# Last stage of a two-layer graph network kernel: operands turned and copied two groups ahead of their products instead of one

## The chip, the cores and the metric

The kernel runs on one core of one Trainium2 chip. The metric is the device time of one launch in microseconds (us). A core has five engines that run their own queues in order: TensorE (PE in the profile, with its weight loads as PEld), VectorE (DVE), ScalarE (ACT), GpSimd (POOL) and SyncE (SP). They meet through semaphores. In this kernel SP and POOL mostly issue DMA transfers: SP the plain ones, POOL the indirect ones, which gather or scatter 128 rows of 96 floats by a list of row numbers.

## The reference

A graph has 50000 nodes with 96 features each and 25000 edges, sorted by their target node `dst`. Two layers follow each other; each adds to its input and normalises.

```python
# layer 0: gated messages, summed per target, then a node update
edge_input = concat([x[src], edge_attr_32])
messages = gelu(edge_input @ mW1 + mb1) @ mW2 + mb2
gates = sigmoid(gelu(edge_input @ gW1 + gb1) @ gW2 + gb2)
aggregated = segment_sum(messages * gates, dst, N)
h = x + gelu(concat([x, aggregated]) @ uW1 + ub1) @ uW2 + ub2
x1 = layernorm(x + layernorm(h) * ln_g + ln_b)

# layer 1: attention over edges, 8 heads of 12 features
K, Q, V = x1 @ Wk + bk, x1 @ Wq + bq, x1 @ Wv + bv
E = edge_attr_96 @ We + be
score = K[src] * Q[dst] / sqrt(12) * E
score = exp(clip(sum over each head of score, -5, 5))
wV = segment_sum(V[src] * score, dst, N)
Z = segment_sum(score, dst, N)
out = layernorm(x1 + wV / (Z + 1e-6))
```

All is float32.

## The kernel before

The kernel has three stages. The edge stage gathers `x[src]` and makes the gated messages; the update stage makes `x1` for all nodes and stores it, with `layernorm(x1)` as the output of nodes that no edge reaches; the last stage, the one that changes, does layer 1 for the edges. It takes 49 groups of 512 edges (`EGROUPS`, four tiles of 128 each, `EJ`). Since edges are sorted by target, a running sum that a mask resets at each new target gives the segment sums, and the row of a target's last edge is scattered to `out`.

POOL's queue is one long list of indirect transfers, 196 of each of five kinds: gathers of `x` (L355), scatters to `agg_d` (L364), gathers of `x1` by target (L380), and, in the last stage, gathers of `x1` by source into a ring of `AHEAD` = 24 groups in the tile `node_work` (L392, `gather_src`) and scatters to `out` (L399, `scatter_out`). In the last stage POOL first issues the gathers of groups 0 to 7, then the scatter of group 0, and from there one gather group and one scatter group in turn: the scatter of group g-7 stands behind the gather of group g (`BEHIND` = 7). After the gather of group 48 the scatters of groups 42 to 48 are left. A gather of group g waits until PE has turned group g-4 (`LEAD`); a scatter of group g waits for `fin_made`, the end of ACT's four operations L667 on that group.

One step of the last stage is called here by its number i, the group whose products it makes. All engines have a function `attend_step(i)` for it.

- PE: wait until ACT has copied all three operands of group i; products K (L545), Q (L546), E (L549) and V (L552), where V waits until the scan of group i-1 is done (`cscanned`); turning the scan of group i-1 back (L556); turning the source rows of group i+1 (L418 with `node_work`) once their gather has landed; the head sums of group i (L538); turning the target rows (L418 with `wide`) and the edge attributes (L418 with `ea`) of group i+1.
- ACT: K with its bias (L663); the four final operations of group i-3 (L667); the three copies of the turned operands of group i+1 out of PSUM (L673, into `nT` or `einT`, the two sets of `opT`); the exponential of the scores of group i (L676), which so stands behind the copies.
- DVE: products with Q (L934) and E (L946), the clip (L969), the score times V (L986), the scan (L992), and between them the division by Z (L952 to L961), the statistics (L980) and the root of groups i-1 and i-2; last `cshift` (L999), which releases L667.
- SP: for each group g the load of its edge attributes `ea` (L327) and then of its mask (L330). The load of `ea` for group g waits until PE has turned group g-2 (there are two buffers), the mask of group g waits for the scan of group g-2. SP's queue is in order, so the load of `ea` for group g+1 stands behind the mask of group g.

PSUM banks 0, 1 and 2 hold the turned source rows, target rows and edge attributes of one group only.

Of the kernel before, what the change touches and what calls it, by code (L numbers as in the profile page):

```python
# [32 lines left out]
EGROUPS = -(-E // EROWS)  # L33
# [11 lines left out]
XSLOTS = 4  # L45
AHEAD = 24
EDGE_LEAD, LEAD, BEHIND = 8, 4, 7
# [27 lines left out]
def build(nc, x, src, dst, ea32, ea96, mW1, mb1, mW2, mb2, gW1, gb1, gW2, gb2, uW1, ub1, uW2, ub2,  # L75
          ln_g, ln_b, Wq, bq, Wk, bk, We, be, Wv, bv, ident_c, heads_c, spare_c, bounds_c, out):
    with ExitStack() as ctx:
# [84 lines left out]
        def two_banks(b):  # L162
            return ps[:, b:b + 2, 0:EJ * D]


        nTf = nT[0:D, :, :].rearrange("p s c -> p (s c)")
        opT = [[nTf[:, 0:512], nTf[:, 512:1024], nTf[:, 1024:1536]],
               [nTf[:, 1536:2048], einT[0:D, 0, :], einT[0:D, 1, :]]]

# [58 lines left out]
        def slot_total(slot):  # L228

            return 16 * len(range(slot, NGROUPS, 2))  # L230
# [185 lines left out]
        def _(pe):  # L416
# [123 lines left out]
            def attend_step(i):  # L540
                s = i % 2
                if 0 <= i < EGROUPS:
                    pe.wait_ge(opsT_copied, i * 3 + 3)
                    xsT, xdT, eaT = opT[s]
                    pe.matmul(ps[0:D, 3, :], Wks[:, :], xsT, start=True, stop=True).then_inc(k_summed, 1)  # L545
                    pe.matmul(ps[0:D, 4, :], Wqs[:, :], xdT, start=True, stop=True).then_inc(q_summed, 1)  # L546
                    if i >= 1:
                        pe.wait_ge(clipped, i)
                    pe.matmul(ps[0:D, 5, :], Wes[:, :], eaT, start=True, stop=True).then_inc(e_summed, 1)  # L549
                    if i >= 1:  # L550
                        pe.wait_ge(cscanned, i)
                    pe.matmul(ps[0:DH, 6, :], Wvs[:, :], xsT, start=True, stop=True).then_inc(v_summed, 1)  # L552
                if i >= 1:
# [3 lines left out]
                    m.then_inc(seg_turned, 1)  # L557
                if i + 1 < EGROUPS:
                    n = i + 1
                    pe.wait_ge(x1s_gathered[n % 2], of_group(n))  # L560
# [11 lines left out]

            for i in range(-1, EGROUPS + 1):
                attend_step(i)
# [3 lines left out]
        def _(act):  # L578
# [80 lines left out]
            def attend_step(i):  # L659
# [4 lines left out]
                if i >= 3:  # L664
# [4 lines left out]
                    o.then_inc(fin_made, 1)  # L669
                if i + 1 < EGROUPS:  # L670
                    for b in range(3):
                        act.wait_ge(ops_turned, i * 3 + 4 + b)
                        act.activation(opT[1 - s][b], ps[0:D, b, :], ACT.Copy).then_inc(opsT_copied, 1)  # L673
                if 0 <= i < EGROUPS:
# [3 lines left out]
            for t in range(2):  # L678
                act.wait_ge(x1_stored[t], slot_total(t))
            for i in range(-1, EGROUPS + 3):  # L680
                attend_step(i)
# [353 lines left out]
```

## Time and profile before

| | |
|---|---|
| median of 3 runs | 1260.01 us (1258.67 to 1260.13) |
| the profiled execution | 1260.09 us, span of the core 1258.3 us |
| PE busy | 959.2 us, 76% |
| DVE busy | 935.4 us, 74% |
| ACT busy | 690.8 us, 55% |
| POOL busy | 945.6 us, 75%, 984 instructions |
| first gather of the last stage (POOL, L392) | 756.52 us |
| first turning in the last stage (PE) | 762.92 us |
| first scatter to `out` (POOL, L399) | 796.49 us |

The times of rows are microseconds from the span's start. Busy shares are averages over three stages; the last stage fills the last 500 us. Idle time of an engine is listed with what ended it; "issue" as what ended it means that the engine waited for nothing that the profile shows. A row that is marked x4 stands for four instructions of one kind in direct succession.

### The profile page before, as it was taken

The numbers are of one execution on the slowest core, as the hardware profiler recorded it, in microseconds if no ns is written. First come the engines' busy times: TensorE is split into PE (matmuls) and PEld (weight loads), VectorE is DVE, ScalarE is ACT, GpSimd is POOL, SyncE is SP. The second block draws the span as 40 slices with busy tenths as digits, with TensorE's granted clock in tenths as the row PEclk, the third lists the DMA queues.
The fourth block names the chain that finished last, engine by engine and source line by source line (L and its number), as shares of the span: only waits on it lengthen the run. The fifth ranks groups of instructions, "written<-read, shape, count | busy, mean of one in ns | idle before, by whom it ended". The sixth has DMA issues, their size and how long they took to land. (4 is left out here: it accounts for less than half of the span.)

```text
span 1258.3 us, 18104 instructions
## 1 busy us (share of the span) xinstructions
PE 959.2 (76%) x4628; PEld 580.5 (46%) x4628; DVE 935.4 (74%) x4244; ACT 690.8 (55%) x1522; POOL 945.6 (75%) x984
## 2 busy tenths in 40 slices
PE   5789999989988898888887006887777786787780
PEld 2334444448777677777675003443333333333330
DVE  3435454547999999999999604999777877787873
ACT  2445555533788888888888703555444443444441
POOL 6677777777777777777777777777777777777777
PEclk9889999999999999999998558999888888788875
DMA  5975555444677777777775432333222322222320
GB/s 126 198 194 182 178 183 182 104 140 128 201 219 226 234 224 222 229 235 220 224 230 175 153 78 65 96 88 86 74 74 74 74 74 74 74 75 73 82 59 29
DMA packets 131946, 178.07 MB, mean 142 GB/s; under 512 B 75125, under 2 KB 76852, under 8 KB 131841
## 3 DMA queue, kind: packets, MB, share of 16 engines
q1 hardware_dynamic: 97741, 130.13, 35.5%
q0 software_dynamic: 31360, 46.18, 14.9%
q10 hardware_dynamic: 2740, 0.60, 0.3%
q8 instruction: 36, 0.59, 0.2%
q14 instruction: 69, 0.57, 0.1%
HBM read 101.31 MB, written 77.56 MB: 142 GB/s over the span
## 5 line engine op out<-in xcount | busy, mean ns | idle before, releaser
L399 POOL DMA_INDIRECT out<-wide,put_at x196 | 192.9, 984 | 59.7 <-issue 57.6
L364 POOL DMA_INDIRECT agg_d<-wide,put_at x196 | 191.2, 976 | 61.9 <-issue 55.5
L355 POOL DMA_INDIRECT wide<-in_x,src_i x196 | 185.5, 946 | 69.5 <-issue 58.1
L392 POOL DMA_INDIRECT node_work<-agg_d,src_i x196 | 188.1, 960 | 59.7 <-issue 57.0
L380 POOL DMA_INDIRECT wide<-agg_d,dst_at x196 | 187.7, 957 | 60.1 <-issue 49.7
L635 ACT ACTIVATE node_work<-node_work,nshift,nscale 128x96 f32<-128x96 f32 x392 | 145.7, 454 | 75.7 <-DVE nshift L885 75.6
L673 ACT ACTIVATE nT<-ps 96x512 f32<-96x512 f32 x99 | 57.0, 592 | 169.5 <-PE ps L418 169.4
L418 PE MATMUL ps<-ident,node_work 128*96 128x128 f32 x196 | 32.9, 293 | 133.7 <-DMA node_work<-agg_d,src_i 133.7
L508 PE MATMUL ps<-uW2s,nT 97*128 97x96 f32 x784 | 98.8, 279 | 45.1 <-ACT nT L653 45.1
L767 DVE SCALAR_TENSOR_TENSOR ps<-hidden,ps 96x512 f32<-96x512 f32 x49 | 33.9, 692 | 128.4 <-ACT hidden L616 128.4
L508 PEld LDWEIGHTS ps<-uW2s,nT 97*128 97x128 f32 x784 | 91.6, 192 | 55.1 <-ACT nT L653 55.1
L641 ACT ACTIVATE node_work<-node_work,nscale 128x96 f32<-128x96 f32 x392 | 112.7, 361 | 0.0
L667 ACT ACTIVATE wide<-yc,cshift,cscale 128x96 f32<-128x96 f32 x196 | 75.5, 456 | 62.7 <-DVE cshift L999 62.2
L850 DVE BATCH_NORM_STATS2 bn<-ps 128x6 f32<-128x96 f32 x392 | 99.3, 258 | 11.3 <-PE ps L508 11.2
L523 PEld LDWEIGHTS ps<-centre,einT 96*128 96x128 f32 x784 | 95.2, 192 | 25.0 <-issue 25.0
L864 DVE SCALAR_TENSOR_TENSOR node_work<-node_work,nscale 128x96 f32<-128x96 f32 x392 | 101.9, 305 | 4.3 <-ACT node_work L635 4.3
L518 PE MATMUL ps<-einT,uW1x 96*96 96x512 f32 x196 | 97.2, 619 | 0.0
L523 PE MATMUL ps<-centre,einT 96*128 96x96 f32 x784 | 94.1, 273 | 0.0
L896 DVE BATCH_NORM_STATS2 bn<-node_work 128x6 f32<-128x96 f32 x392 | 89.4, 249 | 0.0
L545 PE MATMUL ps<-nT,Wks 96*96 96x512 f32 x98 | 61.2, 710 | 35.0 <-ACT nT L673 17.8
L418 PEld LDWEIGHTS ps<-ident,node_work 128*96 128x96 f32 x196 | 21.2, 132 | 139.9 <-issue 78.2
L616 ACT ACTIVATE hidden<-ps,gb2s 96x512 f32<-96x512 f32 x49 | 33.5, 683 | 90.9 <-PE ps L478 90.9
(156 smaller groups left out, 2267.8 us busy)
## 6 DMA issues: line engine op xcount, KB each, us to landing
agg_d<-zeros SPq DMA_DIRECT2D x40, 480.0 KB, 4.3
x_in<-in_x SPq DMA_DIRECT2D x49, 384.0 KB, 3.2
node_work<-agg_d SPq DMA_DIRECT2D x49, 384.0 KB
agg_d<-node_work SPq DMA_DIRECT2D x49, 384.0 KB, 3.5
out<-node_work SPq DMA_DIRECT2D x49, 384.0 KB
mask<-cont_d SPq DMA_DIRECT2D x49, 208.0 KB
mask<-cont_d SPq DMA_DIRECT2D x49, 192.0 KB, 3.3
ea<-in_edge_attr SPq DMA_DIRECT2D x48, 192.0 KB, 3.7
```

Of the source, the lines that this page charges most:

```text
L355: pool.indirect_dma_start(rows[:, g * EJ + j, :], None, x, rows_at(src_i, g, j)).then_inc(xs_gathered[g % 2], 16)
L364: pool.indirect_dma_start(agg_d, rows_at(put_at, g, j), rows[:, g * EJ + j, :], None).then_inc(agg_added[g % 2], 16)
L380: pool.indirect_dma_start(rows[:, g * EJ + j, :], None, x1_d, rows_at(dst_at, g, j)).then_inc(xd_gathered[g % 3], 16)
L392: pool.indirect_dma_start(ahead[:, g % AHEAD, j, :], None, x1_d, rows_at(src_i, g, j)).then_inc(x1s_gathered[g % 2], 16)
L399: pool.indirect_dma_start(out, rows_at(put_at, g, j), rows[:, g * EJ + j, :], None, bounds_check=N - 1, oob_is_err=False).then_inc(out_sca ...
L508: m = pe.matmul(ps[:, 4 + 2 * s + j // 4, (j % 4) * D:(j % 4 + 1) * D], nT[:, s, j * P:(j + 1) * P], uW2s[:, :], start=False, stop=j % 4 == 3)
L518: m = pe.matmul(ps[0:D, 2 + b, :], uW1x[:, :], xT[:, b, :], start=False, stop=True)
L523: m = pe.matmul(ps[:, 4 + 2 * (1 - s) + j // 4, (j % 4) * D:(j % 4 + 1) * D], xT[:, j // 4, (j % 4) * P:(j % 4 + 1) * P], centre[:, :], st ...
L635: o = act.activation(x1o[:, s, j * D:(j + 1) * D], y[:, s, j * D:(j + 1) * D], ACT.Identity, bias=nshift[:, k, j:j + 1], scale=nscale[:, k ...
L641: o = act.activation(oo[:, 1 - s, j * D:(j + 1) * D], x1o[:, 1 - s, j * D:(j + 1) * D], ACT.Identity, scale=nscale[:, k, 2, j:j + 1])
L850: b = dve.bn_stats(bn[:, 0, j, :], ps[:, 4 + 2 * s + j // 4, at:at + D])
L864: b = dve.scalar_tensor_tensor(y[:, s, at], hg[:, s, at], nscale[:, 1 - s, 0, j:j + 1], xb[:, s, at], ALU.mult, ALU.add)
```

## The change

PE turns group i+2 in step i where it turned group i+1, and ACT copies that group in the same step. So the operands of group i are copied one step earlier than before, and since two groups can now be copied and not yet used, there are three sets of copied operands. The third set lies in the last part of `node_work` (`oo`, where the update stage keeps the output rows that it stores), for which the ring of gathered rows shrinks from 24 groups to 20. ACT waits in step 0 until all those stores have landed (`out_stored`). Both engines start with one step more (i = -2). The order on DVE, POOL and SP is unchanged, and so are the conditions of SP's loads; there are still two `ea` buffers.

```diff
-AHEAD = 24
+AHEAD = 20
...
+        ooT = oo[0:D, :, :].rearrange("p s c -> p (s c)")
         opT = [[nTf[:, 0:512], nTf[:, 512:1024], nTf[:, 1024:1536]],
-               [nTf[:, 1536:2048], einT[0:D, 0, :], einT[0:D, 1, :]]]
+               [nTf[:, 1536:2048], einT[0:D, 0, :], einT[0:D, 1, :]],
+               [ooT[:, 0:512], ooT[:, 512:1024], ooT[:, 1024:1536]]]
...
-                    xsT, xdT, eaT = opT[s]
+                    xsT, xdT, eaT = opT[i % 3]
...
-                if i + 1 < EGROUPS:
-                    n = i + 1
+                if i + 2 < EGROUPS:
+                    n = i + 2
+                    if 1 <= n <= 2:
+                        pe.wait_ge(opsT_copied, n * 3)
                     pe.wait_ge(x1s_gathered[n % 2], of_group(n))
...
-            for i in range(-1, EGROUPS + 1):
+            for i in range(-2, EGROUPS + 1):
                 attend_step(i)
...
-                if i + 1 < EGROUPS:
+                if i + 2 < EGROUPS:
+                    if i == 0:
+                        for t in range(2):
+                            act.wait_ge(out_stored[t], slot_total(t))
                     for b in range(3):
-                        act.wait_ge(ops_turned, i * 3 + 4 + b)
-                        act.activation(opT[1 - s][b], ps[0:D, b, :], ACT.Copy).then_inc(opsT_copied, 1)
+                        act.wait_ge(ops_turned, (i + 2) * 3 + 1 + b)
+                        act.activation(opT[(i + 2) % 3][b], ps[0:D, b, :], ACT.Copy).then_inc(opsT_copied, 1)
...
-            for i in range(-1, EGROUPS + 3):
+            for i in range(-2, EGROUPS + 3):
                 attend_step(i)
```

TensorE at the beginning of the last stage before: turnings of group 0 (`node_work`, `wide`, `ea`), its four products, then the turnings of group 1 with the head sums between them.

```order
552 L418 MATMUL ps<-ident,node_work 96x128 x4
553 L418 MATMUL ps<-ident,wide 96x128 x4
554 L418 MATMUL ps<-ident,ea 96x128 x4
555 L545 MATMUL ps<-nT,Wks 96x512
556 L546 MATMUL ps<-nT,Wqs 96x512
557 L549 MATMUL ps<-nT,Wes 96x512
558 L552 MATMUL ps<-nT,Wvs 104x512
559 L418 MATMUL ps<-ident,node_work 96x128 x4
560 L538 MATMUL ps<-hidden,heads 104x512
```

The same place now (line numbers are two higher):

```order
552 L420 MATMUL ps<-ident,node_work 96x128 x4
553 L420 MATMUL ps<-ident,wide 96x128 x4
554 L420 MATMUL ps<-ident,ea 96x128 x4
555 L420 MATMUL ps<-ident,node_work 96x128 x4
556 L420 MATMUL ps<-ident,wide 96x128 x4
557 L420 MATMUL ps<-ident,ea 96x128 x4
558 L547 MATMUL ps<-nT,Wks 96x512
559 L548 MATMUL ps<-nT,Wqs 96x512
560 L551 MATMUL ps<-nT,Wes 96x512
561 L554 MATMUL ps<-nT,Wvs 104x512
562 L420 MATMUL ps<-ident,node_work 96x128 x4
563 L540 MATMUL ps<-hidden,heads 104x512
```

The turnings of group 1 now stand ahead of the products of group 0, and those of group 2 behind them.

TensorE at the end of the stage before, from the products of group 47 on: the last turnings (group 48) stand in step 47.

```order
977 L545 MATMUL ps<-nT,Wks 96x512
978 L546 MATMUL ps<-einT,Wqs 96x512
979 L549 MATMUL ps<-einT,Wes 96x512
980 L552 MATMUL ps<-nT,Wvs 104x512
981 L556 MATMUL ps<-ident,seg 128x104 x4
982 L418 MATMUL ps<-ident,node_work 96x128 x4
983 L538 MATMUL ps<-hidden,heads 104x512
984 L418 MATMUL ps<-ident,wide 96x128 x4
985 L418 MATMUL ps<-ident,ea 96x128 x4
986 L545 MATMUL ps<-nT,Wks 96x512
```

The same end now, from the last turnings on:

```order
976 L420 MATMUL ps<-ident,node_work 96x128 x4
977 L540 MATMUL ps<-hidden,heads 104x512
978 L420 MATMUL ps<-ident,wide 96x128 x4
979 L420 MATMUL ps<-ident,ea 96x128 x4
980 L547 MATMUL ps<-node_work,Wks 96x512
981 L548 MATMUL ps<-node_work,Wqs 96x512
982 L551 MATMUL ps<-node_work,Wes 96x512
983 L554 MATMUL ps<-node_work,Wvs 104x512
984 L558 MATMUL ps<-ident,seg 128x104 x4
985 L540 MATMUL ps<-hidden,heads 104x512
986 L547 MATMUL ps<-nT,Wks 96x512
```

Behind the last turnings there are now the products of two groups, 47 and 48, where there was one.

## Rows read from the trace of the kernel before

**Rows 1.** The page, busy us, share and instructions of each engine.

```profile
PE 959.2 (76%) x4628; PEld 580.5 (46%) x4628; DVE 935.4 (74%) x4244; ACT 690.8 (55%) x1522; POOL 945.6 (75%) x984
```

**Rows 2.** Groups of instructions, POOL, 640 us to the end: count | busy, mean ns | idle before.

```profile
L399 POOL DMA_INDIRECT out<-wide,put_at x196 | 192.9, 984 | 59.7 <-issue 57.6 <-DMA out<-wide,put_at 2.1
L392 POOL DMA_INDIRECT node_work<-agg_d,src_i x196 | 188.1, 960 | 59.7 <-issue 57.0 <-DMA out<-wide,put_at 2.1 <-PE ps L418 0.6
```

**Rows 3.** Timeline, POOL: start us, us, what [idle before it <-what ended it].

```profile
765.27 0.94 POOL L392 DMA_INDIRECT node_work<-agg_d,src_i  x1 [0.30 <-issue]
...
770.27 0.95 POOL L392 DMA_INDIRECT node_work<-agg_d,src_i  x1 [0.30 <-issue]
...
796.49 1.01 POOL L399 DMA_INDIRECT out<-wide,put_at  x1 [0.30 <-issue]
...
806.73 1.01 POOL L399 DMA_INDIRECT out<-wide,put_at  x1 [0.30 <-issue]
```

**Rows 4.** Timeline, ACT, final operations of group 0.

```profile
791.63 1.54 ACT L667 ACTIVATE wide<-yc,cshift,cscale 128x96 f32<-128x96 f32 x4 [1.51 <-DVE cshift L999]
```

**Rows 5.** The chain that ended last, a piece at the start of the stage.

```profile
760.27 2.51 DMA node_work<-agg_d,src_i
```

**Rows 6.** Timeline, PE, start of the stage (groups 0, 1 and 2).

```profile
762.92 1.06 PE L418 MATMUL ps<-ident,node_work 128*96 128x128 f32 x4 [77.51 <-DMA node_work<-agg_d,src_i]
...
766.37 1.10 PE L545 MATMUL ps<-nT,Wks 96*96 96x512 f32 x2 [0.68 <-ACT nT L673]
...
769.88 0.60 PE L418 MATMUL ps<-ident,node_work 128*96 128x128 f32 x4
...
779.98 0.60 PE L418 MATMUL ps<-ident,ea 128*96 128x128 f32 x4
```

**Rows 7.** Timeline, PE after an idle stretch in mid-stage.

```profile
983.32 0.64 PE L418 MATMUL ps<-ident,node_work 128*96 128x128 f32 x4 [1.68 <-DMA node_work<-agg_d,src_i]
...
985.17 1.06 PE L418 MATMUL ps<-ident,wide 128*96 128x128 f32 x4
```

**Rows 8.** The chain that ended last, a product at low clock.

```profile
1020.15 1.71 PE ps L546 x2
```

**Rows 9.** Timeline, DVE: scans of groups 0 and 1, score times V of groups 1 and 2.

```profile
775.66 1.22 DVE L992 TENSOR_TENSOR_SCAN seg<-mask,ps 104x512 f32<-104x512 f32 x1
...
781.81 0.76 DVE L986 SCALAR_TENSOR_TENSOR ps<-ps,bvs,score 104x512 f32<-104x512 f32 x1
...
789.27 0.75 DVE L986 SCALAR_TENSOR_TENSOR ps<-ps,bvs,score 104x512 f32<-104x512 f32 x1
```

**Rows 10.** Timeline, ACT: exponentials of groups 1 and 2.

```profile
781.15 0.62 ACT L676 ACTIVATE score<-hidden 104x512 f32<-104x512 f32 x1
...
788.15 0.62 ACT L676 ACTIVATE score<-hidden 104x512 f32<-104x512 f32 x1
```

**Rows 11.** Timeline, SP: the load of `ea` for group 3.

```profile
777.28 0.38 SPq L327 DMA_DIRECT2D ea<-in_edge_attr  x1
```

**Rows 12.** The view of line 327, its last line.

```profile
DMA to landing us min/median/max: 3.5/3.7/5.2
```

**Rows 13.** Busy time by stretch: us, PE, PEld, DVE, ACT, POOL, PEclk, DMA.

```profile
766.00:772.00 6.00, 5.63 (x22) 2.88 (x22) 2.11 (x3) 1.77 (x4) 4.48 (x6) 1.00 0.31 72
...
800.00:880.00 80.00, 66.57 (x265) 31.96 (x263) 78.83 (x366) 44.92 (x93) 60.80 (x64) 1.00 0.37 91
```

**Rows 14.** Timeline of the end: scan of group 46, last `ea` turned, scan of group 48.

```profile
1214.57 1.28 DVE L992 TENSOR_TENSOR_SCAN seg<-mask,seg,ps 104x512 f32<-104x512 f32 x1
...
1219.72 0.60 PE L418 MATMUL ps<-ident,ea 128*96 128x128 f32 x4
...
1230.15 1.28 DVE L992 TENSOR_TENSOR_SCAN seg<-mask,seg,ps 104x512 f32<-104x512 f32 x1
```

**Rows 15.** Timeline of the end: final operations and first scatter of group 47.

```profile
1236.89 1.54 ACT L667 ACTIVATE wide<-yc,cshift,cscale 128x96 f32<-128x96 f32 x4 [3.62 <-DVE cshift L999]
...
1246.79 0.97 POOL L399 DMA_INDIRECT out<-wide,put_at  x1 [0.30 <-issue]
```

## The prediction

> **What bounds the kernel now.** First the busy shares: no engine is above 76% [rows 1], which says little, since POOL's rows leave out its pause between two transfers. So next the list of groups with what ended their idle time, for POOL from 640 us on: the 196 scatters and the 196 gathers of the last stage have 59.7 us of idle time each, 57.6 and 57.0 of it "issue", which is 0.30 us ahead of each; what stands beside a DMA or PE is a few times the same 0.30 [rows 2, 3]. POOL waits for nobody. One transfer costs 0.97 + 0.30 = 1.27 us, and a group with its four gathers and four scatters takes 806.73 - 796.49 = 10.24 us [rows 3]. POOL's queue from the first gather of this stage to the last scatter is the path that sets the end, and the rest of the stage matters only where it makes POOL wait. That is at two waits: a gather of group g for the turning of group g-4, and a scatter of group g for its final operations on ACT. The third reading is how much time those waits have to spare.
>
> At the start the first scatter is issued at 796.49, and the final operations of group 0 end at 791.63 + 1.54 = 793.17 [rows 3, 4]. With the 0.30 us that a POOL instruction takes to begin, 3.0 us are spare. From there POOL takes 10.24 us a group and the compute engines 789.27 - 781.81 = 7.5 [rows 9], so the margin grows by 2.7 us with each group, until PE has caught up with the gathers at about 880 us. At the end the scatters come every 5.1 us, and the nearest is group 47: final operations end at 1236.89 + 1.54 = 1238.43, the scatter is issued at 1246.79 [rows 15]. With 0.30 taken off, 8.1 us are spare.
>
> **What the change removes.** In step i of before PE waits for ACT's last copy, 0.68 us ahead of product K [rows 6]. That wait goes. It is worth nothing: between 800 and 880 us, where PE has not yet caught up, DVE is busy 78.83 of 80 us [rows 13], so DVE sets the length of a step; in the later part PE waits for gathers, 1.68 us at 983.32 [rows 7], and so for POOL. No transfer and no arithmetic is added or removed, and the wait for the stored outputs on ACT ends long before. If a shorter step did reach POOL, it could only take away waits, and POOL has none.
>
> **What it moves, at the start.** Ahead of the products of group 0 PE now turns group 1. The last gather of group 0 is issued at 760.27 and has landed 2.51 us later, and PE starts 0.14 after that, at 762.92 [rows 5, 6]. Group 1's last gather is issued at 765.27 [rows 3], so PE can turn it at 765.27 + 2.51 + 0.14 = 767.92. Before, K of group 0 began at 766.37 and the next turning, behind all four products, at 769.88, so the four products take 3.51 [rows 6].
>
> - At full clock three turnings (0.43 each, from 0.60 less the overlap) and the products end at 767.92 + 1.3 + 3.5 = 772.7. Then PE needs group 2, whose last gather is issued at 770.27 [rows 3] and can be turned at 772.92: 3.0 us later than 769.88.
> - All at low clock the turnings take 2.6 (1.06 less overlap each, rows 6) and each product 1.71 [rows 8], so 767.92 + 2.6 + 6.9 = 777.4: 7.5 later. The clock was full in the stretch of before in which PE worked without a pause [rows 13].
> - I take a value near the first. Now PE pauses from 765.7 to 767.9, 2.2 us. After the pause of 1.68 us in mid-stage the first turnings took 0.64 and the next 1.06 [rows 7], so the clock fell to 1.2 GHz for a few us. The like of it here costs about 1.5 us over the full-clock sum: next turning at 774.3, which is 4.4 later.
>
> The Trainium skill, page "TensorE: Matmul & The Clock Gate", section "What's actually happening", says that "the default state is throttled, and activity releases the throttle". By it the added pause at 765.7 speaks against the change, and the sum would lean to the 4.4; were the clock to stay up, it would be the 3.0.
>
> **What it moves, in each step: the edge attributes.** SP's queue now hurts. The load of `ea` for group i+2 stands behind the mask of group i+1, which waits for the scan of group i-1. Before, that load was for the next step. Now PE turns it in the very step in which it is issued. In before the scan of group 0 ended at 775.66 + 1.22 = 776.88, the load behind it was issued at 777.28, 0.40 later, and loads land 3.7 us after issue [rows 9, 11, 12]: 4.1 us after the scan, 4.2 with PE's start. PE reached the turning of `ea` at 779.98 [rows 6], 3.1 after the scan. So PE and behind it ACT's last copy and the exponential come 1.1 us later. In step 1 nothing covers that: the exponential ended at 781.77 and DVE took it at 781.81 [rows 9, 10]. In step 2 the exponential ended at 788.77 and DVE, still at its statistics, took it at 789.27, so 0.5 is covered and 0.6 left [rows 9, 10]. With landings of 3.5 these are 0.9 and 0.4; with 5.2 they are 2.6 and 2.1.
>
> Group 0's final operations stand behind the scan of group 2, and so behind all three: 793.17 + 4.4 + 1.1 + 0.6 = 799.3, and POOL begins 0.30 later, 799.6 instead of 796.49. POOL stalls 3.1 us. Everything behind in its queue comes 3.1 later, and with no idle time in it nothing is won back. The gathers' wait gets easier, as turnings come a step earlier.
>
> **In mid-stage** a group's final operations are one step of 10.24 us later against its gather. Before, the margin of the scatters grew from 3.0 by 2.7 a group over the eight groups to 880 us, to about 25 us; less one step, an estimated 15 us stay spare. The late `ea` has cover there, as PE waits for the gather anyway.
>
> **What it moves, at the end.** When the last gather has landed, PE has the products of two groups before it instead of one. One step without new gathers takes from scan to scan: 1231.43 for group 48, less 1215.85 for group 46, over two, 7.8 us [rows 14]. The last `ea` is late as well: 4.2 after 1215.85, and 0.4 for the issue of the second of its two parts [rows 11], is 1220.4, against 1219.72, so 0.7 [rows 14]. Together 8.5 us against 8.1 spare: POOL stalls 0.4 us at group 47. Bounds: 0 with a step as short as at the start (7.5), and 2 with a landing of 5.2 and half-clock head sums.
>
> **Sum.** 3.1 + 0.4 = 3.5 us on the profiled execution's 1260.09, 1263.6 us. That execution stands 0.1 us from the median of the runs, 1260.01. From the bounds: 0 + 0 at least (3.0 us late, no wait for `ea`), and 7.5 + 2.6 + 2.1 - 3.0 = 9.2, with 2 at the end some 11, at most.
>
> **Rivals.**
> 1. *The margin holds, no change.* The clock stays at 2.4 GHz and `ea` lands before PE asks for it, for example since it moves with less traffic beside it. Then the lateness is 3.0 us against 3.0 spare, the end fits, and the time is 1260.1; with half of the `ea` wait, 1261. For it: the margin is as large as the smallest lateness. Against it: no landing under 3.5 [rows 12]. Whole range to 1262.5: 33%.
> 2. *Not slower but faster.* The removed 0.68 us of each step shortens the steps ahead of the first scatter, the products of groups 1 and 2 come early, and DVE, whose order lets it take them, ends each scan sooner; from three steps on (2.0 us) that would pay for the `ea` waits. It would be a gain only if pauses of POOL shrank too, at most the 2.1 + 2.1 + 0.6 = 4.8 us that are listed beside a DMA or PE [rows 2]: 1255.3. Against it: DVE's 78.83 of 80 [rows 13]. 4%.
> 3. *A long stall.* The products of group 0 run fully at 1.2 GHz (+3.1 over my value), or loads of `ea` land after 5 us in both steps (+3.0). The stall is 6 us and the time 1266.5. For it: the one landing of 5.2 [rows 12]. 10%.
> 4. *Steps longer than POOL's.* If `ea` stretched each step beyond 10.24 us, the spare 15 us would be used up from an excess of 0.4 us a step over 40 steps; at 1 us it would cost 25 us, 1285. Against it: a step of 7.5 plus 1.1 is 8.6. 1%.
>
> My forecast, a stall of 2.5 to 5 us, has the other 52%.
>
> **Range and chances.** 0.2% is 2.5 us, about what a measurement of this kernel can tell from no change, so the bound for slower is 1262.5. The forecast and rivals 3 and 4 lie above it, 63%, less 2 for noise: slower 61%. Rival 1 and that noise: same 35%. Faster 4%. The range of 8 in 10 goes from 1260.3, which leaves out part of rival 1, to 1266.8, which takes in most of rival 3.
>
> **What the profile of the changed kernel would show.** The first scatter (L401 there) near 799.6 with over 2 us of idle time ahead that ends with ACT; the first K near 769.3 in place of 766.37; PE's turnings of `ea` at 780 to 880 us released by the DMA, about 1 us each, and scans some 8.1 apart in place of 7.5; POOL's pauses of 0.30 as before from 810 us on; at the end one pause of half a us ahead of the scatters of groups 46 or 47. A first scatter at 796.5 would make the forecast wrong, and so would landings of `ea` that PE does not wait for.

## The result: 7.8 us slower, where 3.5 was forecast

| | before | changed |
|---|---|---|
| median of 6 runs | 1260.36 us (1258.67 to 1261.54) | 1268.12 us (1265.89 to 1269.47) |
| ratio of times, 95% interval | | 1.0058 (1.0048 to 1.0069) |
| profiled execution | 1260.09 us | 1265.89 us, the fastest of the six |
| first gather of the last stage to last scatter, POOL | 499.20 us | 506.29 us |

The forecast was 1263.6 us with a range to 1266.8: the sign was right, the size too small, and the median lies outside the range. Since the stages ahead of the last one vary by a few us from execution to execution, the measure used from here on is the length of POOL's queue in the last stage, from the start of its first gather to the start of its last scatter. The queue holds the same transfers as before, and POOL's busy time in the whole kernel has not grown (944.3 us for 945.6), so what this length gains over before is pauses. It gained 7.09 us.

The page of the changed kernel has nearly the same busy shares [rows 1]:

```profile
PE 967.7 (77%) x4628; PEld 593.1 (47%) x4628; DVE 939.1 (74%) x4244; ACT 688.7 (54%) x1522; POOL 944.3 (75%) x984
```

The list of what POOL waited for in the last stage (engine, tile and line, what ended the wait: us in total, times, longest) has one entry of more than a few pauses of 0.30 that before does not have, the one with ACT's final operations L671:

```profile
POOL out L401 <- issue: 57.3, 188, 0.3
POOL node_work L394 <- issue: 56.1, 184, 0.3
POOL out L401 <- ACT wide L671: 8.3, 3, 5.4
```

Its 8.3 us in 3 waits are two stalls and one of the usual pauses of 0.30. POOL's timeline shows where they lie (start, duration, what, and in brackets the idle time ahead and what ended it). The first row is the stage's first gather; then come the first scatters of group 0, of group 1 and, near the end, of group 46, and the last scatter of the stage:

```profile
755.23 0.95 POOL L394 DMA_INDIRECT node_work<-agg_d,src_i  x1 [0.30 <-issue]
...
800.23 1.01 POOL L401 DMA_INDIRECT out<-wide,put_at  x1 [5.35 <-ACT wide L671]
...
810.47 1.00 POOL L401 DMA_INDIRECT out<-wide,put_at  x1 [0.30 <-issue]
...
1247.47 0.97 POOL L401 DMA_INDIRECT out<-wide,put_at  x1 [2.62 <-ACT wide L671]
...
1261.52 0.97 POOL L401 DMA_INDIRECT out<-wide,put_at  x1 [0.30 <-issue]
```

Less the usual 0.30 these stalls are 5.05 and 2.32 us, together 7.4, and the stage grew by 7.1. Forecast were 3.1 and 0.4. Between them POOL goes on at its old pace: the first scatter of the next group comes at 810.47, 10.24 us behind, as before [rows 3].

### Where the first stall comes from

The mark to read this by is the end of each scan, counted from the first gather of the stage (756.52 before, 755.23 now), since the final operations of group 0 stand behind the scan of group 2. DVE's timeline of the changed kernel, the scans of groups 0, 1 and 2 [rows 9]:

```profile
779.49 1.22 DVE L999 TENSOR_TENSOR_SCAN seg<-mask,ps 104x512 f32<-104x512 f32 x1
...
788.10 1.28 DVE L999 TENSOR_TENSOR_SCAN seg<-mask,seg,ps 104x512 f32<-104x512 f32 x1
...
796.18 1.28 DVE L999 TENSOR_TENSOR_SCAN seg<-mask,seg,ps 104x512 f32<-104x512 f32 x1
```

| us | before | changed | later by | forecast |
|---|---|---|---|---|
| scan of group 0 ends | 20.36 | 25.48 | 5.12 | 4.4 |
| from there to scan 1 | 7.00 | 8.67 | 1.67 | 1.1 |
| from there to scan 2 | 7.46 | 8.08 | 0.62 | 0.6 |
| together | | | 7.41 | 6.1 |

TensorE's timeline from its start in the stage gives the first two rows [rows 6]:

```profile
761.63 1.06 PE L420 MATMUL ps<-ident,node_work 128*96 128x128 f32 x4 [76.31 <-DMA node_work<-agg_d,src_i]
...
767.26 0.61 PE L420 MATMUL ps<-ident,node_work 128*96 128x128 f32 x4 [2.87 <-DMA node_work<-agg_d,src_i]
...
768.26 1.06 PE L420 MATMUL ps<-ident,ea 128*96 128x128 f32 x4
769.11 1.92 PE L547 MATMUL ps<-nT,Wks 96*96 96x512 f32 x2
770.82 1.33 PE L548 MATMUL ps<-nT,Wqs 96*96 96x512 f32 x2
...
773.70 0.60 PE L420 MATMUL ps<-ident,node_work 128*96 128x128 f32 x4
...
780.76 1.17 PE L554 MATMUL ps<-nT,Wvs 96*104 96x512 f32 x2 [2.15 <-DVE seg L999]
...
783.27 1.91 PE L540 MATMUL ps<-hidden,heads 96*104 96x512 f32 x2
...
785.47 0.60 PE L420 MATMUL ps<-ident,ea 128*96 128x128 f32 x4
...
793.56 0.64 PE L420 MATMUL ps<-ident,ea 128*96 128x128 f32 x4 [0.93 <-DMA ea<-in_edge_attr]
```

PE waits 2.87 us for the gathers of group 1, and then runs for some us at the lower of its two clock levels: a turning takes 1.06 against 0.60 and K 1.92 against 1.10 before. The turning of group 2 begins 12.07 us after PE's start in the stage, before it was 769.88 - 762.92 = 6.96. So 5.11 of the lateness is there. It has two parts. From the turning of group 1 to that of group 2 PE takes 773.70 - 767.26 = 6.44, of which I had 6.4. The rest is the gather itself, as the chain of waits shows (start, duration, what):

```profile
763.97 3.16 DMA node_work<-agg_d,src_i
```

I had the last gather of group 1 land 2.51 us after its issue, as that of group 0 did [rows 5]. It took 3.16, 0.65 more. That this can be so stood in the trace of before too, where nothing waited for it; the view of L392 there, from 755 to 775 us, ends with

```profile
DMA to landing us min/median/max: 2.4/2.5/3.2
```

In step 1 PE waits 2.15 us for the scan of group 0 ahead of V. That wait stood in the order of before too, but was shorter, and no half clock came behind it:

```profile
776.94 1.11 PE L552 MATMUL ps<-nT,Wvs 96*104 96x512 f32 x2 [1.17 <-DVE seg L992]
```

Now it comes: head sums of 1.91 where those at full clock take 1.02. PE reaches the turning of `ea` at 785.47, 4.8 us after the end of the scan of group 0, with no wait in front of it: the load had landed. From V to the turning of `ea` PE takes 785.47 - 780.76 = 4.71 us, where it took 779.98 - 776.94 = 3.04 before, 1.67 less. So the 1.67 us of this step are the slow clock, and the late `ea` that the prediction named is covered by it. In step 2 PE does wait for `ea`, 0.93 us, and starts on it 793.56 - 789.38 = 4.18 us after the scan, as forecast (4.2).

The granted clock from 781 to 785 us, behind the wait of 2.15 us in step 1 (columns as in [rows 13]: us, PE, PEld, DVE, ACT, POOL, PEclk, DMA), is 0.58, near the lower level, 1.2 of 2.4 GHz:

```profile
781.00:785.00 4.00, 4.00 (x13) 2.17 (x13) 2.39 (x8) 0.59 (x1) 2.98 (x4) 0.58 0.53 140
```

The Trainium skill, page "TensorE: Matmul & The Clock Gate", section "What's actually happening", has the throttled clock as the default and activity as what lifts it. The trace agrees in so far as the pauses of 2.87 and 2.15 us were each followed by a stretch at 1.2 GHz. But the length of the last pause alone does not tell it. In step 5 of the same execution PE waits 1.81 us for `ea`, and the granted clock from 820 to 825 us is 1.00:

```profile
819.50 0.64 PE L420 MATMUL ps<-ident,ea 128*96 128x128 f32 x4 [1.81 <-DMA ea<-in_edge_attr]
```

Of the 7.41 us the spare 3.02 is taken off, which leaves 4.4, and the stall is 5.05. The difference is in POOL itself. ACT's operations [rows 4] end late now, and POOL takes up its scatter 0.94 us after their end and not 0.30:

```profile
797.75 1.54 ACT L671 ACTIVATE wide<-yc,cshift,cscale 128x96 f32<-128x96 f32 x4 [1.83 <-DVE cshift L1006]
...
1245.07 1.54 ACT L671 ACTIVATE wide<-yc,cshift,cscale 128x96 f32<-128x96 f32 x4 [3.34 <-DVE cshift L1006]
```

They end at 799.29 and 1246.61, the scatters begin at 800.23 and 1247.47, so 0.94 and 0.86. The 0.30 that I used is the pause between two POOL instructions of which the second needn't wait. With 0.64 more the sum is 7.41 - 3.02 + 0.64 = 5.03.

### Where the second stall comes from

The scatter that stalls is that of group 46, whose final operations stand behind the scan of group 48, the last one. Counted from the issue of the last gather (1214.83 before, 1218.31 now) the scans of groups 46, 47 and 48 end after 1.02, 8.92 and 16.60 us before, and after 10.56, 18.43 and 26.33 now. So the last is 9.73 us late, one step of 7.9 and 1.8 more, where I had one of 7.8 and 0.7. The 8.1 us spare were read at group 47; group 46 had the same before (its final operations ended at 1233.26, its scatter was issued at 1241.68). Less these and with the late start again, here 0.86 - 0.30 = 0.56, 2.2 us are left, and 2.3 were measured. Here is PE's timeline at the last turnings (the `ea` turning of before is in [rows 14]), and behind it the stretch with its granted clock, columns as in [rows 13]:

```profile
1221.57 0.72 PE L420 MATMUL ps<-ident,node_work 128*96 128x128 f32 x4 [0.96 <-DMA node_work<-agg_d,src_i]
1222.08 1.91 PE L540 MATMUL ps<-hidden,heads 96*104 96x512 f32 x2
1223.79 1.06 PE L420 MATMUL ps<-ident,wide 128*96 128x128 f32 x4
1224.64 0.98 PE L420 MATMUL ps<-ident,ea 128*96 128x128 f32 x4
```

```profile
1222.00:1225.00 3.00, 3.00 (x10) 1.72 (x9) 1.79 (x11) 0.71 (x2) 2.23 (x3) 0.50 0.14 45
```

A pause of 0.96 us ahead of the turnings, and the whole piece runs at 1.2 GHz: 1.91 for the head sums, 1.06 and 0.98 for the turnings. From the first of these turnings to K they take 1225.45 - 1221.57 = 3.88 us, some 1.7 more than at full clock. PE does not wait for the last `ea`: its second part was issued at 1219.89, and PE comes to it 4.75 us later.

How late the end is in the order of before differs between executions too. The last scan ended 16.60 us after the last gather's issue in the profiled execution of before, and 18.67 in that of run B below, which has the same order on PE and also turned its last group at the lower clock (0.96 and 1.06).

### The profile page after: what moved, and what is told of

It is laid out like the page before. It is cut to its first block and busy times, and to the rows that moved or that the text cites. A ratio compares the mean times of both kernels' runs of the same rounds, so it can differ in the third digit from the quotient of the medians.

```text
span 1264.1 us, 18107 instructions
## 1 busy us (share of the span) xinstructions
PE 967.7 (77%) x4628; PEld 593.1 (47%) x4628; DVE 939.1 (74%) x4244; ACT 688.7 (54%) x1522; POOL 944.3 (75%) x984
## 5 line engine op out<-in xcount | busy, mean ns | idle before, releaser
L420 PE MATMUL ps<-ident,node_work 128*96 128x128 f32 x196 | 41.1, 348 | 132.5 <-DMA node_work<-agg_d,src_i 132.5
L671 ACT ACTIVATE wide<-yc,cshift,cscale 128x96 f32<-128x96 f32 x196 | 75.5, 456 | 87.9 <-DVE cshift L1006 87.9
L680 ACT ACTIVATE nT<-ps 96x512 f32<-96x512 f32 x67 | 39.3, 592 | 128.3 <-PE ps L420 127.3
L420 PEld LDWEIGHTS ps<-ident,node_work 128*96 128x96 f32 x196 | 26.0, 155 | 138.9 <-issue 80.3
L420 PEld LDWEIGHTS ps<-ident,wide 128*128 128x128 f32 (+1 forms) x392 | 56.6, 155 | 71.0 <-issue 63.9
L976 DVE TENSOR_SCALAR hidden<-ps 104x512 f32<-104x512 f32 x49 | 33.6, 687 | 70.5 <-PE ps L540 70.5
```

Of the source, the lines that this page charges most:

```text
L420: mmx = pe.transpose(to, of, ident[:, :])
```

## The experiments

My theory was: POOL's queue sets the end, its stalls are lateness less margin at two places, and all else is hidden. The rivals: the step in mid-stage got dearer (late `ea`, a smaller ring), or a queue that the profile does not show. "Stage" is the length from first gather to last scatter in the profiled execution, "stalls" are POOL's pauses less 0.30, at the start and at the end. Stage and stalls are from one execution each. Ratios are to before on the same chip.

| | ratio, 95% interval | stage | stalls |
|---|---|---|---|
| before | | 499.20 | none |
| changed | 1.0058 (1.0048 to 1.0069) | 506.29 | 5.05, 2.32 |
| A, changed, scatters a group further behind | 1.0004 (0.9993 to 1.0015) | 499.05 | 0.32, 0 |
| B, before with the same | 0.9999 (0.9989 to 1.0010) | 498.73 | none |
| C, before, scatters a group nearer | 1.0046 (1.0028 to 1.0063) | 501.75 | 2.69, 0 |
| D, two ahead from step 10 on | 1.0017 (1.0008 to 1.0027) | 501.53 | 0, 2.56 |
| E, two ahead up to step 40 | 1.0035 (1.0022 to 1.0048) | 504.49 | 5.05, 0 |
| F, `ea` ahead of the mask | 1.0058 (1.0044 to 1.0072) | 504.43 | 5.36, 0.28 |
| G, PE kept busy in its waits | 1.0045 (1.0031 to 1.0058) | 503.76 | 3.07, 1.35 |
| H, F and G | 1.0028 (1.0017 to 1.0039) | 500.95 | 1.47, 0.67 |
| I, two ahead in steps 10 to 39 only | 1.0001 (0.9989 to 1.0012) | 498.94 | none |
| J, before, scatters two groups nearer | 1.0128 (1.0104 to 1.0152) | 512.44 | 9.32, 1.23, 0.14, 2.56 |
| K, D with PE kept busy at the end | 1.0011 (0.9999 to 1.0022) | 500.62 | 0, 1.74 |
| L, K and F | 1.0009 (0.9997 to 1.0021) | 499.40 | 0.24, 0.34 |

### A, B and C: the margin alone

The order of scatters against gathers on POOL is one number; A sets it in the changed kernel, B and C in the one before.

```diff
-EDGE_LEAD, LEAD, BEHIND = 8, 4, 7
+EDGE_LEAD, LEAD, BEHIND = 8, 4, 8      # A, B;  6 in C
```

> The changed kernel with the scatters one group further behind the gathers (8 instead of 7), so each scatter comes about 5.1 us later in POOL's queue against the gathers. Theory (the loss is two stalls of POOL, 5.0 us at the first scatter and 2.3 us at group 46): both margins grow by 5.1, so the first stall falls to about 0 and the second to 0; no POOL pause over 0.4 us in the last stage, total within 1.5 us of the kernel before, 7 us under the changed one. Rival (the loss is spread over the stage, by slower transfers or by steps that are longer): the pauses go, but the time stays near +7 us.

> The kernel before with the scatters 8 groups behind. Control. Theory: POOL never waited, so more margin is worth nothing: within 1.5 us of the kernel before. Rival (a larger distance is of use by itself, so that the run above mixes two effects): faster by more than 2.5 us.

> The kernel before with the scatters only 6 groups behind, turning and copying as before. Theory: each margin shrinks by 5.1 us. At the start 3.0 spare less 5.1 is a stall of 2.1, and about 0.6 more since a wait that ends late costs POOL about 0.9 us and not 0.30: first pause ahead of a scatter 2.7 us above the usual 0.30; at the end 8.1 less 5.1 leaves 3 us, no stall. Total +2.7 us. Rival (the changed placement of turnings costs by itself and margins play no part): no difference, 0 us.

A took the whole loss away: 1260.81 us, with one pause of 0.62 ahead of its first scatter.

```profile
802.59 1.01 POOL L401 DMA_INDIRECT out<-wide,put_at  x1 [0.62 <-issue]
```

A and B have the same order on POOL and differ in the change alone: 499.05 and 498.73, with no stall in B. So with the margin there, the change costs nothing in the middle, and the wait of 0.68 us that it removes from each step wins nothing either. Both were forecast. C is the opposite, the order before with four gathers' time (5.0 us) less of margin:

```profile
794.71 1.01 POOL L399 DMA_INDIRECT out<-wide,put_at  x1 [2.99 <-ACT wide L667]
```

Its scan of group 0 ended 20.25 us after the first gather and the steps took 6.99 and 7.63, so the lateness is 0.05 and the account says 5.0 - 3.02 + 0.64 + 0.05 = 2.7; measured 2.69. The median lies 5.5 us above before and the stage only 2.6, to which I come back under J.

### D, E and I: the two places one at a time

A table `TURNED` tells for each step which groups are turned and copied in it. Both engines go by it, and ahead of each turning PE waits for the copies of the group before.

```diff
+    reach = i + (2 if TWO_FROM <= i < TWO_TO else 1)
...
-                if i + 2 < EGROUPS:
-                    n = i + 2
+                for n in TURNED[i]:
```

with `TWO_FROM, TWO_TO` = 10, 49 in D, -2, 40 in E and 10, 40 in I.

> The changed kernel, but turning only one group ahead until step 9; in step 10 two groups are turned, from there two ahead as in the changed kernel, to the end. Theory: the stall at the first scatter goes (as in the kernel before), the one at the end, 2.3 us at group 46, stays: total +2.3 us (1.5 to 3.5) against the kernel before. Rival (loss spread over the stage): nearly the whole +7 us stays, since 39 of 49 steps are as in the changed kernel. Rival (the stall at the end is a result of the late start): it goes too, +0.

> The changed kernel, but from step 40 on only one group ahead again (step 40 turns none). Theory (two separate stalls): the stall at the first scatter stays, 5.0 us, the one at the end goes. From the first gather of the last stage to the last scatter 504.2 us in the profiled execution, against 499.2 of the kernel before and 506.3 of the changed one; total +5 us. Rival (loss spread over the stage): about +7 us, as 42 of the 49 steps are unchanged.

> The changed kernel with two groups ahead only in steps 10 to 39, one ahead at both ends. Theory (the whole loss is two stalls, at the first scatter and at group 46): no pause of POOL over 0.4 us, 499.2 us from the first gather to the last scatter as before, total within 1.5 us of the kernel before. Rival (some of the loss is spread over mid-stage): 30 of 49 steps are as in the changed kernel, so +4 us stays.

D has the first scatter on time and the second stall only, E the reverse:

```profile
1247.32 0.97 POOL L407 DMA_INDIRECT out<-wide,put_at  x1 [2.86 <-ACT wide L677]
```

```profile
801.42 1.01 POOL L407 DMA_INDIRECT out<-wide,put_at  x1 [5.35 <-ACT wide L677]
```

The stages grew by 2.33 and 5.29, together 7.6 against 7.1 with both. So the two places are separate and add up. I, two ahead in 30 of 49 steps and one ahead at both ends, has no wait for ACT in POOL's list at all, and the time of before. The first line of that list:

```profile
POOL out L407 <- issue: 57.9, 190, 0.3
```

### F, G and H: is it `ea` or the clock?

F issues the load of `ea` for group g+1 ahead of the mask of group g, so it no longer stands behind the scan. G has PE do idle work in its waits: 20 transposes of the identity into a PSUM bank that holds nothing yet in step -1, ahead of group 1's turning, and 18 in step 1 ahead of V.

```diff
+            ea_load(0)
             for g in range(EGROUPS):
+                if g + 1 < EGROUPS:
+                    ea_load(g + 1)              # F, H
...
+                if i == -1:
+                    spin(20)                    # G, H
...
+                    if i == 1:
+                        spin(18)                # G, H: ahead of V's wait
```

> The changed kernel with SP's queue reordered: the load of the edge attributes of group g+1 stands ahead of the mask of group g, so it no longer waits for a scan. Theory (the late load cost 0.6 us in step 2; in step 1 the half clock of TensorE made PE come later than the load anyway): first stall 4.4 us in place of 5.0, PE never waits for the load, the end unchanged at 2.3; first gather to last scatter 505.7. Rival (the late edge attributes, 15.7 us of PE's waits in all, are the chief cause): the stalls shrink by 2 us or more, to under 504.3.

> The changed kernel with extra turnings of the identity into an unused bank, 20 in the pause ahead of group 1 and 18 in that ahead of V of group 1, which keep TensorE busy so that its clock does not fall; nothing reads them. Theory: the products of group 0 and the head sums of group 1 run at 2.4 GHz; the turning of group 2 comes 0.7 us earlier and step 1 is 0.6 us shorter (the late edge attributes then set it), so the first stall is 3.8 us in place of 5.0; the end unchanged; first gather to last scatter 505.0. Rival (the clock has no part, only orders do): 506.3 and a stall of 5.0.

> Both: the extra turnings and the edge attributes ahead of the mask. Theory: what is left of the first stall is group 0's products behind the turning of group 1, which waits for group 1's gather: scan of group 0 about 4.4 us later than before, step 1 of 7.0 and step 2 of 7.5 as before; against 3.0 spare and 0.6 for a late wait that is a stall of 2.0 us. The end stays at 2.3; first gather to last scatter 503.4. Rival (the two are not additive, another wait takes over, as DVE's): 504.5 or more.

In F the step from scan 1 to scan 2 went from 8.08 back to 7.39 us, so the 0.62 of that step is the load. The step from scan 0 to scan 1 stayed at 8.67: there the load isn't what is late. The first stall did not shrink (5.36): scan 0 ended 26.47 after the first gather, since PE found the gathers of group 1 only 3.66 us after the last one's issue and ran its turnings of group 1 slow as well (1.06 us each). The second stall fell to 0.28, which I had not expected: the last scan ended 24.39 us after the last gather's issue in place of 26.33. Most of that is the clock, which was up at the last turnings there (head sums 1.02 for 1.91): from the last group's first turning to the end of scan 46 it takes 5.80 us, as in before, and 7.30 in the changed kernel. The changed kernel doesn't wait for the last `ea`, so the load can't be what it lost there. Nothing in F keeps PE busy at the end, so a single execution doesn't show that the edit brought the clock up.

```profile
806.79 1.01 POOL L407 DMA_INDIRECT out<-wide,put_at  x1 [5.66 <-ACT wide L677]
...
1251.87 0.97 POOL L407 DMA_INDIRECT out<-wide,put_at  x1 [0.58 <-issue]
```

In G the steps are 8.12 and 7.88 us and scan 0 ends at 24.29, 3.09 us of stall by the account and 3.07 measured. I had expected 3.8 and an end unchanged at 2.3. The end was 1.35, though nothing is changed there: the last turnings ran at full clock in this execution too, and PE waited 0.36 us for the last `ea`, which is what that load costs at the end with the clock up. PE's timeline shows the products at full clock behind the idle work (L546 are the transposes of the identity, L553 is K):

```profile
769.52 3.71 PE L546 MATMUL ps<-ident 128*128 128x128 f32 x20
...
774.38 1.02 PE L553 MATMUL ps<-nT,Wks 96*96 96x512 f32 x2
```

```profile
803.59 1.01 POOL L401 DMA_INDIRECT out<-wide,put_at  x1 [3.37 <-ACT wide L679]
...
1250.25 0.97 POOL L401 DMA_INDIRECT out<-wide,put_at  x1 [1.65 <-ACT wide L679]
```

H has both, and both steps are those of before, 6.99 and 7.52. What is left, 24.10 for scan 0, is 3.74 us late, and the stall 1.47 (account: 1.41). Expected were 4.4 and 2.0, and 2.3 at the end, where 0.67 came, again with the last turnings at full clock:

```profile
796.40 1.01 POOL L407 DMA_INDIRECT out<-wide,put_at  x1 [1.77 <-ACT wide L685]
```

So the 7.41 us ahead of the first stall divide as follows. From the turning of group 1 to that of group 2 H takes 4.75 us, all at full clock, and the changed kernel 6.44: 1.7 us are the clock in group 1's turning and the products of group 0. The other 3.4 of scan 0 are the wait for group 1's gathers with its turning (forecast 3.0 with a landing of 2.51; it was 3.16 here, and 3.47 in H). In step 1 the 1.7 are the clock and, once that is up, 1.1 of them the load, as G shows. The 0.6 in step 2 are the load.

### J: one margin smaller again

> The kernel before with scatters only 5 groups behind, nothing else changed. Theory of margins: 10.2 us less at each end. Start: 3.0 spare less 10.2, and 0.6 for a late wait, is a stall of 7.8 us. End: 8.1 less 10.2 and 0.6 is 2.7 us. First gather to last scatter 499.2 + 10.5 = 509.7. Rival (a stall at the start is won back or the second wait absorbs the first): 507 or less.

```diff
-EDGE_LEAD, LEAD, BEHIND = 8, 4, 7
+EDGE_LEAD, LEAD, BEHIND = 8, 4, 5
```

```profile
795.32 1.01 POOL L399 DMA_INDIRECT out<-wide,put_at  x1 [9.62 <-ACT wide L667]
...
797.86 1.00 POOL L399 DMA_INDIRECT out<-wide,put_at  x1 [1.53 <-issue]
...
1254.46 0.97 POOL L399 DMA_INDIRECT out<-wide,put_at  x1 [2.86 <-ACT wide L667]
```

The stage grew by 13.24 and the pauses are 9.32 + 1.23 + 0.14 + 2.56 = 13.25, so all of the growth is pauses. What ended the 1.23 ahead of the second scatter the profile doesn't show, and its cause stays open. The first is larger than 10.0 - 3.02 + 0.64 = 7.6 by 1.7, since scan 0 ended 22.13 us after the first gather here and not 20.36, in the order of before. PE shows why, K and Q of group 0:

```profile
765.88 2.02 PE L545 MATMUL ps<-nT,Wks 96*96 96x512 f32 x2 [0.68 <-ACT nT L673]
767.69 1.92 PE L546 MATMUL ps<-nT,Wqs 96*96 96x512 f32 x2
```

They ran at 1.2 GHz, where in the profiled execution of before K took 1.10 [rows 6]. The clock at the stage's start thus differs between executions of the same instructions: of the eight traces with this order on PE at the start, six have scan 0 end 20.25 to 20.36 us after the first gather, J 22.13 and L 23.04. With margin to spare that doesn't show in the time. Once the margin is gone each execution's lateness should go into its time. That fits with the medians of C and J, which lie 5.5 and 17.7 us above before where the stages of their profiled executions grew by 2.6 and 13.2; that this is the reason for those medians is an inference from one trace each.

### K and L: the clock at the end

K is D with 6 idle transposes ahead of V's wait and 10 ahead of the gather's wait in steps 44 to 46; L has the order of F besides. The idle work goes into bank 0, so PE waits for ACT's copies ahead of it.

```diff
+                    if 44 <= i <= 46:
+                        pe.wait_ge(opsT_copied, i * 3 + 6)
+                        spin(6)                 # ahead of V's wait
...
+                    if 44 <= i <= 46:
+                        spin(10)                # ahead of the gather's wait
```

> Two groups ahead from step 10 (no stall at the start, 2.6 us at the end when run without more), with extra turnings of the identity in the pauses of steps 44 to 46, into a bank that the next turning overwrites, so that TensorE's clock stays up when the last gather lands. Theory (of the 2.3 to 2.6 at the end about 1.2 come from head sums and turnings at 1.2 GHz): scan of group 46 ends 9.4 us after the last gather's issue in place of 10.7, stall at the end 1.3. Rival (the late edge attributes make the stall, not the clock): 2.3 or more.

> The same with the load of the edge attributes ahead of the mask too. Theory: scan of group 46 ends 8.9 us after the last gather's issue, as in the kernel before; what is left is one more step of 7.8 us against 8.1 spare and 0.6 for a late wait: stall at the end 0.3 to 0.8. Rival (clock alone): as the run beside it.

```profile
1241.93 0.97 POOL L407 DMA_INDIRECT out<-wide,put_at  x1 [2.04 <-ACT wide L686]
```

```profile
798.19 1.01 POOL L413 DMA_INDIRECT out<-wide,put_at  x1 [0.54 <-issue]
...
1243.37 0.97 POOL L413 DMA_INDIRECT out<-wide,put_at  x1 [0.64 <-issue]
```

In K the last scan ended 25.87 us after the last gather's issue (D: 26.72), and the stall fell from 2.56 to 1.74, less than I expected (1.3). In L it ended after 24.49, and the stall was 0.34, as forecast. The load of `ea` doesn't explain the 1.4 us between them. Here are the first and the last turning of the last group, in K and then in L:

```profile
1217.54 0.64 PE L426 MATMUL ps<-ident,node_work 128*96 128x128 f32 x4 [0.49 <-DMA node_work<-agg_d,src_i]
...
1219.32 0.60 PE L426 MATMUL ps<-ident,ea 128*96 128x128 f32 x4
```

```profile
1219.34 0.64 PE L432 MATMUL ps<-ident,node_work 128*96 128x128 f32 x4 [1.55 <-DMA node_work<-agg_d,src_i]
...
1221.12 0.60 PE L432 MATMUL ps<-ident,ea 128*96 128x128 f32 x4
```

PE waits for the last `ea` in neither. It begins the first turning 4.17 us after the last gather's issue in K (issued at 1213.37) and 3.15 in L (1216.19), so 1.0 of the 1.4 us is the landing of that gather, and from there to scan 46 both take 5.8 us. The rest lies in the two steps behind it, in which PE ran slow at different places (head sums of group 48 2.04 in K and 1.11 in L). In D that gather was late too (4.22), and from it to scan 46 D took 6.47, so most of the 0.85 us from D to K (0.7) is the clock there. L's small pause at the start, 0.24, is a start of the order of before at low clock, scan 0 ending after 23.04 us.

No version beats the kernel before. A, B, I, K and L can't be told from it, and nothing in the change could make them faster, as POOL has no wait to lose.

## Why the prediction was right and wrong

- *POOL's queue is the path, and the time grows by its stalls alone.* Right: in all twelve versions and the changed kernel, stage growth and stalls agree within 0.5 us, in the changed kernel and in C, E and J within 0.3.
- *The removed wait of 0.68 us is worth nothing.* Right: A against B. In the stretch from 800 to 880 us, where I had DVE as the bound [rows 13], it was busy less than before, since with the late `ea` the steps were 7.9 to 9.2 us long (7.6 to 7.8 before); with POOL's 10.24 us for a group that cost nothing.

```profile
800.00:880.00 80.00, 64.51 (x250) 30.86 (x247) 74.38 (x338) 41.88 (x86) 60.88 (x63) 0.98 0.32 82
```

- *Group 2's turning 4.4 us later.* Mis-sized: 5.1. The sum from the turning of group 1 on, with 1.5 for the clock, was right (6.44 for 6.4; against H the clock costs 1.7). The landing of 2.51 us was wrong: I took one row for all gathers, and the 3.16 of this one made the pause 2.87 where I had 2.2.
- *`ea` 1.1 us late in step 1.* The load was priced right: G, with the clock up, has the step 1.12 longer. But in the changed kernel it isn't what is waited for. The step was 1.67 longer by the clock after V's wait (2.15 us where it was 1.17), a term that the prediction put at nothing. That most of the size came out is luck: the slow clock hid the load. I had looked for what SP delays in that step and not for where PE pauses in it.
- *0.6 in step 2.* Right, in cause and size: F removed it.
- *3.0 us spare.* Right; C confirms it to 0.1 us.
- *POOL begins 0.30 after ACT's end.* Wrong at both stalls: 0.94 and 0.86. 0.30 is the distance of an instruction that had nothing to wait for. In sum 1.2 us of the loss.
- *The end: 8.5 late against 8.1 spare.* Mis-sized: 9.7. The step was 7.9 (forecast 7.8), but the rest 1.8 for 0.7, and by another cause: the last turnings ran at 1.2 GHz behind a pause of 0.96 us, and PE didn't wait for the last `ea`, for which the 0.7 stood. I had slow head sums only in the upper bound. The stall came at group 46 and not at 47; both had 8.1 us spare.
- *Nothing in mid-stage (15 us spare).* Right: I. In the changed kernel 17.8 to 20.7 us were spare from group 11 to group 41.

At the first stall the 1.9 us too few are 0.65 of the landing, 0.6 of step 1 and 0.64 of POOL's late start; the second stall's 1.9 are 1.1 by which the clock at the last turnings cost more than the 0.7 set down for `ea`, 0.1 of the step, 0.56 of the late start, and the rest small differences. All have one direction, and they fall on a difference: an error of 1.3 in a lateness of 6.1 is two fifths of the 3.1 that the margin leaves. The rival of the long stall had this mechanism and 6 us, at 10%. It needed only terms that lay within their bounds to add up, in two places, and should have had about as much as the forecast. Last, the median of the changed kernel is 2.2 us above its own profiled execution, to which all of this account belongs. The last stage began 1.3 us earlier in that execution than in the one of before (755.23 and 756.52), by work that the change doesn't touch. The rest, under 1 us, may be a start that is later in other executions, as in J; no trace shows that.

## What to carry to other kernels

Where one in-order queue sets the time and never waits, read each of its dependences as a margin, at the first and the last group above all, and price a change of order as lateness less margin, with the error of the lateness kept whole; a deeper lead fills and empties a pipeline one step longer at each end. Busy shares hide such a queue. The Trainium skill, page "Perfetto Trace Analysis", section "Identifying the Most-Contended Engine", has one optimise the engine of highest occupancy first, and sets TensorE's matmul share aside as no good measure. By [rows 1] that names POOL with 75%, but by one point over DVE with 74%, though it is POOL alone whose pauses moved the length of the stage about one for one. If such a change is wanted for another reason, widen the distance in the queue with it: one number (A) took back the 7.8 us, as far as the measurement can tell.

## What the runs showed of the chip

- An indirect DMA on POOL whose wait ends late started 0.85 to 0.94 us after the end of ACT's last operation, in all 18 pauses above 0.33 us ahead of a group's first scatter; one whose wait is over when its turn comes, 0.30 after the one ahead.
- Pauses of PE of 0.96, 2.15 and 2.87 us were each followed by some us at 1.2 GHz, in which head sums took 1.91 us for 1.02 and K 1.92 for 1.02. Pauses of 1.81 us in the changed kernel and 1.17 in before were not, so a pause's length alone doesn't tell what clock follows.
- With the same instructions the first group's products ran at full clock in one execution (K 1.10) and at half in another (2.02), which moved the first scan by 1.8 us, from 20.36 to 22.13, and in L, with the same order on PE there, by 2.7. The Trainium skill, page "TensorE: Matmul & The Clock Gate", section "What's actually happening", says of TensorE's warm-up that "it's run-variable", and these traces agree.
- Keeping PE busy with idle transposes in its waits brought the clock back (K 1.02 in G) and gained 2.0 us of the first stall.
- Gathers of one size mostly landed 2.5 us after their issue (the median), but up to 4.2 in the changed kernel and 4.8 in D; the last one, which the end of the stage waits for, 3.2 in the changed kernel and 4.1 in D and K. Why some come late was not tried.
